# Gamma and beta as PSUM rows, a shared adapter bank, and one instruction list per engine for layer 0 and the seam

## What is computed

```python
# layer 0: adapter of the batch's language, then LayerNorm with its gamma and beta
h = relu(x @ W1[lang] + b1[lang]); v = x + h @ W2[lang] + b2[lang]
c = (v - mean(v)) * rsqrt(var(v) + 1e-5) * gamma[lang] + beta[lang]
x = x + bitlinear(gelu(bitlinear(c, W1f, b1f)), W2f, b2f)      # 256 -> 1024 -> 256
# layer 1: linear of the batch's subject, then a feed-forward with a convolution over tokens
y = x @ W[subj].T + b[subj]
x = x + bit_linear(silu(conv3(bit_linear(y, w1)) + conv_b), w2)
# bitlinear: W -> clip(round(W / mean|W|), -1, 1) * mean|W|; x -> round(x * 127 / max|x|) * max|x| / 127
```

## Time and profile before

| what | us |
|---|---|
| median of 3 runs | 321.74 |
| lowest and highest | 318.56 and 323.08 |
| span of the profiled execution | 319.6 |
| VectorE busy | 276.6 |
| TensorE busy (matmul) | 264.5 |
| GpSimd busy | 259.2 |
| ScalarE busy | 240.6 |

### The profile page before, as it was taken

The page is one execution under the profiler, slowest core; times in us unless marked ns, Lnnn a source line. Parts: engine busy times, 40 slices in busy tenths (PEclk is TensorE's granted clock), DMA queues, the critical chain, the costliest instruction groups (busy, mean ns, idle before and its releaser), DMA issues. The chain is left out here.

```text
span 319.6 us, 6460 instructions
## 1 busy us (share of the span) xinstructions
PE 264.5 (83%) x1676; PEld 179.7 (56%) x1700; DVE 276.6 (87%) x606; ACT 240.6 (75%) x366; POOL 259.2 (81%) x402
## 2 busy tenths in 40 slices
PE   6679878869798887999889797989899898967574
PEld 6234334535455454566656665868587686745452
DVE  0778988896899989955899999999999999999671
ACT  4588897966776487567566888889989888978770
POOL 2567899996898988759999999998989799898310
PEclk9977799999999999999999999999999999999997
DMA  7995773579496368454430333445436373444764
GB/s 249 320 363 118 222 197 76 113 159 213 100 215 126 75 87 178 69 100 91 44 66 2 60 74 66 118 98 91 111 93 122 70 98 82 101 98 100 120 145 115
DMA packets 90745, 39.50 MB, mean 124 GB/s; under 512 B 73005, under 2 KB 88141, under 8 KB 90710
## 3 DMA queue, kind: packets, MB, share of 16 engines
q1 hardware_dynamic: 84532, 30.47, 46.8%
q10 hardware_dynamic: 6178, 8.62, 8.6%
HBM read 18.11 MB, written 4.19 MB: 70 GB/s over the span
## 5 line engine op out<-in xcount | busy, mean ns | idle before, releaser
L812 POOL TENSOR_TENSOR raw_all<-raw_all,mid 128x1024 f32<-128x1024 f32 x32 | 63.7, 2000 | 0.7 <-DVE raw_all L1025 0.7
L548 ACT ACTIVATE g<-banks,dqz 128x1024 f32<-128x1024 f32 x32 | 35.5, 1112 | 24.4 <-POOL r L757 21.2
L805 POOL TENSOR_SCALAR mid<-apad,taps,convb 128x512 f32<-128x512 f32 x64 | 48.8, 774 | 0.5 <-DVE apad L1018 0.5
L608 ACT ACTIVATE banks<-apad,taps 128x512 f32<-128x512 f32 x64 | 42.3, 682 | 6.9 <-DVE apad L1018 6.8
L970 DVE TENSOR_REDUCE am<-g 128x1 f32<-128x1024 f32 x32 | 38.6, 1211 | 8.6 <-ACT g L548 8.5
L1025 DVE SCALAR_TENSOR_TENSOR raw_all<-apad,taps,banks 128x512 f32<-128x512 f32 x64 | 45.8, 743 | 0.0
L1018 DVE TENSOR_TENSOR apad<-banks,dqb 128x512 f32<-128x512 f32 x64 | 40.9, 684 | 4.6 <-PE banks L1337 4.5
L757 POOL TENSOR_SCALAR r<-g,qs 128x1024 uint16<-128x1024 f32 x32 | 36.8, 1153 | 6.2 <-DVE qs L982 5.9
L1365 PE MATMUL banks<-tern,q1T 128*128 128x256 bf16 x256 | 33.8, 276 | 9.5 <-DMA q1T<-r 8.0
L1227 PE MATMUL banks<-tern,qT 128*128 128x512 bf16 x117 | 36.6, 388 | 5.5 <-ACT qcT L540 3.3
L627 ACT ACTIVATE r<-g,qs 128x1024 uint16<-128x1024 f32 x32 | 36.6, 1144 | 5.3 <-DVE qs L1044 3.2
(11 more groups left out here) (116 smaller groups left out, 561.5 us busy)
## 6 DMA issues: line engine op xcount, KB each, us to landing
out_y<-xs SPq DMA_DIRECT2D x32, 128.0 KB, 2.0
xs<-in_x ACTq DMA_DIRECT2D x7, 512.0 KB, 5.7
x2T<-in_xT ACTq DMA_DIRECT2D x4, 512.0 KB, 5.2
wl<-in_cwl SPq DMA_DIRECT2D x8, 256.0 KB, 2.7
xT<-in_xT ACTq DMA_DIRECT2D x3, 512.0 KB, 4.2
raw_all<-in_w1a ACTq DMA_DIRECT2D x1, 1024.0 KB, 5.0
cw<-in_cw SPq DMA_DIRECT2D x16, 64.0 KB, 5.0
gam<-in_gamma SPq DMA_DIRECT2D x8, 128.0 KB, 3.0
```

Of the source, the lines that this page charges most:

```text
L608: act.activation(bank(BANK_U[g % 3]), apad[:, f, 2:S + 2], ACT.Copy, scale=taps[:, f, 2:3]).then_inc(p_last, 1)
L805: pool.tensor_scalar(mid[f // 2 % 2][:, f % 2, :], apad[:, f, 1:S + 1], taps[:, f, 1:2], convb[:, f:f + 1], ALU.mult, ALU.add).then_inc(p_ ...
L812: pool.tensor_tensor(c[:, 2 * q:2 * q + 2, :], c[:, 2 * q:2 * q + 2, :], mid[q % 2][:, :, :], ALU.add).then_inc(p_sum, 1)
```

## The change

1. Gamma and beta. The two tables (10 languages by 256) are loaded once into SBUF (load_affine), with the ids on 10 partitions (load_langs). VectorE compares the ids with a row number (choose_languages). TensorE's affine_columns multiplies the tables by the chosen columns, ScalarE copies the result to affineT, and for each batch TensorE's affine_rows transposes a broadcast column into one PSUM bank (BANK_GB, 7), from which centre and normalise read gamma and beta. The bank has one buffer: affine_rows(b) waits for normalise(b-1,1), and centre waits for affine_rows.
2. The adapter. adapter_in writes to BANK_AD, too, and waits for add_adapted of both pairs of the batch before (until now for the relu alone).
3. scale_z is two operations of one element instead of one of two elements with a stride.
4. Order. Layer 0, the seam and the first batches of layer 1 are one list for each engine (first); slot2 has a new order and runs for s = 3 to 8; the rest is a list (ending). The orders of all engines are new throughout.

```diff
-        gam = [sb(f"gam{k}", [P, D]) for k in range(2)]
-        bet = [sb(f"bet{k}", [P, D]) for k in range(2)]
+        affine = sb("affine", [L, 2, D])
+        affineT = sb("affineT", [P, 2 * KD, B])
+        row_of = sb("row_of", [L, 1])
+        langs = sb("langs", [L, B], I32)
+        chosen = sb("chosen", [L, B])
...
-        amz = [sb(f"amz{k}", [P, 2, 2])[:, :, 0] for k in range(2)]
-        sz = [sb(f"sz{k}", [P, 2, 2])[:, :, 0] for k in range(2)]
+        amz = [sb(f"amz{k}", [P, 2]) for k in range(2)]
+        sz = [sb(f"sz{k}", [P, 2]) for k in range(2)]
...
-        BANK_AD, BANK_DN, BANK_QT, BANK_UP, BANK_IN = 0, 1, 2, 3, 7
+        BANK_AD, BANK_DN, BANK_QT, BANK_UP, BANK_GB = 0, 1, 2, 3, 7
+        columns = bank(BANK_GB)[:, 0:2 * KD * B].rearrange("p (c b) -> p c b", b=B)
+        gam = bank(BANK_GB)[:, 0:D]
+        bet = bank(BANK_GB)[:, D:2 * D]
...
-        def run(opening, slot1, closing, slot2):
-            opening()
-            for s in range(5, B + 1):
-                slot1(s)
-            closing()
-            for s in range(3, B + 4):
+        def run(first, slot2, ending):
+            first()
+            for s in range(3, B + 1):
                 slot2(s)
+            ending()
...
-            def load_norm(b):
...
+            def load_langs():
+                sp.dma_start(langs[:, :], t["ids0"].to_broadcast([L, B])).then_inc(s_langs, 16)
+
+            def load_affine():
+                sp.dma_start(affine[:, 0, :], t["gamma"]).then_inc(s_ldgb, 16)
+                sp.dma_start(affine[:, 1, :], t["beta"]).then_inc(s_ldgb, 16)
...
             def slot2(s):
...
+                on(store2, s - 7, 3)
+                on(store2, s - 6, 1)
+                on(store2, s - 5, 0)
+                on(store2, s - 5, 2)
+                on(transpose2, s - 1, 3)
+                on(transpose2, s, 0)
+                on(transpose2, s, 1)
+                on(transpose2, s, 2)
...
+            load_langs()
+
+            def first():
+                load_adapter_weights(0); load_table(); load_weights(1); load_weights(2); load_second(0); load_ids()
+                load_weights(3); load_first_tokens(); load_affine(); load_adapter_weights(1); load_second(1)
...
+            def ending():
+                store2(2, 3); store2(4, 0); store2(3, 1); store2(4, 2); store2(3, 3); store2(5, 0); store2(5, 2)
+                store2(4, 1); store2(4, 3); store2(5, 1); store2(5, 3); store2(6, 1); store2(6, 0); store2(6, 2)
+                store2(7, 0); store2(6, 3); store2(7, 1); store2(7, 2); store2(7, 3)
...
+            def affine_columns():
+                act.wait_ge(s_gbc, 1)
+                act.activation(affineT[:, :, :], columns, ACT.Copy).then_inc(s_gbT, 1)
...
+            def first():
+                load_tokens(1); weight_sum(0); identities(); load_rows(1); bias_leading(); adapter_hidden(0)
+                load_rows(2); affine_columns(); weight_sum(1); squares(0, 0); squares(0, 1); adapter_hidden(1)
+                bias_middle(); load_rows(3); scaled_weights(1); load_tokens(2); round_z(0, 0); squares(1, 0)
+                untranspose_z(0, 0); round_z(0, 1); squares(1, 1); ternary(1); adapter_hidden(2); gelu(0, 0)
...
+            pool.iota(row_of[:, :], pattern=[[0, 1]], base=0, channel_multiplier=1,
+                      allow_small_or_imprecise_dtypes=True).then_inc(s_rowof, 1)
...
+                bias_table(); negative_mean(0, 0); bias_rest(); negative_mean(0, 1); inverse_deviation(0, 0)
...
+            def choose_languages():
+                dve.wait_ge(s_langs, 16)
+                dve.wait_ge(s_rowof, 1)
+                dve.tensor_scalar(chosen[:, :], langs[:, :], row_of[:, 0:1], None, ALU.is_equal).then_inc(s_chosen, 1)
...
             def centre(b, p):
                 dve.wait_ge(s_nmean[p], b + 1)
-                dve.wait_ge(s_ldgb[b % 2], 32 * (b // 2 + 1))
+                dve.wait_ge(s_gb, b + 1)
...
-                                                   in1=gam[b % 2][:, :], op0=ALU.add, op1=ALU.mult)
+                                                   in1=gam, op0=ALU.add, op1=ALU.mult)
...
-                                                   in1=bet[b % 2][:, :], op0=ALU.mult, op1=ALU.add)
+                                                   in1=bet, op0=ALU.mult, op1=ALU.add)
...
-                dve.tensor_scalar(sz[p], amz[p], QEPS, 1.0 / QMAX, ALU.max, ALU.mult).then_inc(s_sz, 1)
+                for k in range(2):
+                    ins = dve.tensor_scalar(sz[p][:, k:k + 1], amz[p][:, k:k + 1], QEPS, 1.0 / QMAX, ALU.max, ALU.mult)
+                ins.then_inc(s_sz, 1)
...
+            def first():
+                choose_languages(); weight_scale(0); ternary(0); add_adapted(0, 0); centre(0, 0); add_adapted(0, 1)
+                weight_scale(1); normalise(0, 0); absmax_z(0, 0); centre(0, 1); scale_z(0, 0); inverse_z(0, 0)
...
+            def affine_columns():
+                pe.wait_ge(s_ldgb, 32)
+                pe.wait_ge(s_chosen, 1)
+                for c in range(2 * KD):
+                    ins = pe.matmul(columns[:, c, :], affine[:, c // KD, (c % KD) * P:(c % KD + 1) * P], chosen[:, :],
+                                    start=True, stop=True)
+                ins.then_inc(s_gbc, 1)
+
+            def affine_rows(b):
+                if b == 0:
+                    pe.wait_ge(s_gbT, 1)
+                    pe.wait_ge(s_ldid, 16)
+                wait(pe, s_z, pair(b - 1, 1))
+                for c in range(2 * KD):
+                    ins = pe.transpose(bank(BANK_GB)[:, c * P:(c + 1) * P],
+                                       affineT[:, c, b:b + 1].to_broadcast([P, P]), id32[:, :])
+                ins.then_inc(s_gb, 1)
...
             def adapter_in(b):
                 par = b % 2
                 pe.wait_ge(s_ldT[par], 32 * (b // 2 + 1))
-                wait(pe, s_relu, b)
+                wait(pe, s_xx, pair(b - 1, 1))
...
+            def first():
+                weight_total(0); adapter_in(0); affine_columns(); adapter_out(0, 0); affine_rows(0); adapter_out(0, 1)
+                adapter_in(1); weight_total(1); adapter_out(1, 0); adapter_out(1, 1); transpose_z(0, 0)
...
```

More of the change, by code:

```diff
@@ L235, in bank_x @@
         def bank_x(b):
-            return BANK_IN if b == 0 else 0
+            return 0
         def bank_y(b):
-            return BANK_AD if b == 0 else 2
+            return BANK_GB if b == 0 else 2
         BANK_U = [3, 4, 7]
@@ L451, in _ @@
+            def ending():
+                store2(2, 3); store2(4, 0); store2(3, 1); store2(4, 2); store2(3, 3); store2(5, 0); store2(5, 2)
+                store2(4, 1); store2(4, 3); store2(5, 1); store2(5, 3); store2(6, 1); store2(6, 0); store2(6, 2)
+                store2(7, 0); store2(6, 3); store2(7, 1); store2(7, 2); store2(7, 3)
+            run(first, slot2, ending)
             sp.wait_ge(p_st[0], 32 * B)
@@ L677, in _, with ending @@
+            def ending():
+                silu(6, 3); round2(6, 2); silu(7, 0); round2(6, 3); silu(7, 1); round2(7, 0); silu(7, 2); round2(7, 1)
+                silu(7, 3); round2(7, 2); round2(7, 3)
+            run(first, slot2, ending)
         @block.gpsimd
@@ L896, in _, with ending @@
+            def ending():
+                scale_of_down(6, 2); scale_of_down(6, 3); scale_of_down(7, 0); scale_of_down(7, 1)
+                scale_of_down(7, 2); scale_of_down(7, 3)
+            run(first, slot2, ending)
         @block.vector
@@ L1083, in slot2 @@
-            def slot2(s):
+            def slot2(s):
+                on(scale2, s - 3, 1)
+                on(final2, s - 4, 2)
+                on(first_tap, s - 2, 6)
+                on(dequant, s - 2, 7)
+                on(inverse2, s - 3, 1)
+                on(absmax2, s - 3, 2)
+                on(first_tap, s - 2, 7)
+                on(dequant, s - 1, 0)
+                on(final2, s - 4, 3)
+                on(dequant, s - 1, 1)
+                on(scale2, s - 3, 2)
+                on(first_tap, s - 1, 0)
+                on(dequant, s - 1, 2)
+                on(inverse2, s - 3, 2)
+                on(absmax2, s - 3, 3)
+                on(first_tap, s - 1, 1)
+                on(dequant, s - 1, 3)
+                on(first_tap, s - 1, 2)
+                on(scale2, s - 3, 3)
+                on(absmax_y, s)
@@ L1170, in weight_total @@
                 if n >= 2:
-                    wait(pe, s_relu, len(batches))
+                    wait(pe, s_xx, pair(len(batches) - 1, 1))
                     totals.append(n)
@@ L1243, in down1 @@
                 ins.then_inc(s_dn, 1)
-            def slot1(s):
-                on(adapter_in, s)
-                on(up1, s - 3, 3)
-                on(transpose_z, s - 2, 0)
-                once(s, B, transpose_x, 0, 0)
-                on(adapter_out, s, 0)
-                on(down1, s - 4, 3)
-                once(s, B, transpose_x, 0, 1)
-                on(up1, s - 2, 0)
-                on(down1, s - 3, 0)
-                on(transpose_z, s - 2, 1)
```

(10 more changed lines are left out.)

481 lines of the change are left out of this document (202 added, 279 removed).

## The result

| | us |
|---|---|
| before, median of 4 runs (range) | 321.59 (318.56 to 323.08) |
| after, median of 4 runs (range) | 342.16 (341.85 to 344.12) |
| ratio after / before, 95% interval | 1.067 (1.059 to 1.075) |
| profiled execution after: its own time, span | 342.19, 340.4 |

The change makes the kernel 6.7% slower, 340.4-319.6=20.8 us by the spans. The forecast was 320.7 with a range of 309 to 331, so it was wrong, and outside its range. What failed most was the term for layer 1, which the prediction put at 0: it measured +8.0 us; the opening and the end came out 5.5 and 4.2 us above their terms.

What follows compares the result with a forecast made beforehand. Layer 0 was taken to have no single limit (VectorE, GpSimd and TensorE close together), layer 1 to be bound by VectorE. 319.6+11-9-6+3=318.6, plus 2.1 around the span, gave 320.7 us, range 309 to 331.

Steps and rivals of the forecast that it cites:

- the term for layer 1: Layer 1's rearranged slots: VectorE busy 109.3 of 110 us, so nothing to win; 0.
- the opening: Start, up to gelu(1,0): tokens and gamma/beta tables land later behind weight loads, so gelu(1,0) begins near 61; +11 us.
- the end: After the last transpose: 19 stores stand behind it on SP instead of 3; +3 us.
- relief let through in layer 0: Layer 0 after 50 us: TensorE and GpSimd let through three quarters of VectorE's remaining 12 us relief; -9 us.
- longer lists, seam and layer 1: Longer lists recover 6 us of VectorE's idle time in the seam and elsewhere after 50 us; layer 1 itself 0.
- the stretches: VectorE's centring, normalising and scale, lengthened by exclusion with GpSimd, return to unstretched times; 17.9 us together with issue gaps.
- rival 3: VectorE's lengthened operations have another source and stay so; time also 330 us; chance 5%.
- four small products, ScalarE's copy and the adapter's product: Opening chain after gamma and beta land at 24 us; puts the first adapter sum at about 25.5 us.
- VectorE's weight_scale(1) is part of the price: Opening: weight_scale(1) stands ahead of normalise(0,0) and waits behind adapter_in(1); first normalising near 32.5 us.
- 0.4 us a store: End: assumed SP issue time per store, giving 10.8 us after the last transpose's issue, +3.2 us.
- Rival 2: Single buffers make batches wait, 1.3 us in each of seven, 9 us, cancelling the relief; time 330.7 us; chance 22%.
- my sign: Test against single-buffer waits: TensorE's waits for z and xx under 3 us in all; over 8 would mean they bite.

Runs made afterwards that it cites:

- e1: Changed kernel with SP's opening list alone reordered: second adapter weights, gamma/beta and batch 0's tokens issued ahead of the three big weight loads; 329.76 us, ratio to before 1.030.
- e1b: e1 with weight 1's steps moved back behind the first normalising on three engines and affine_columns behind adapter_out(0,0); 332.42 us.
- h1: Changed kernel's operations in the instruction lists of the kernel before, with table loads, column products and row transposes put in; 320.29 us, ratio to before 0.998.
- e8: New lists with the loads of e1, but every layer 1 operation, stores and transposes included, in the old order; 322.69 us, ratio 1.004.
- e13: Changed kernel with e1's loads and e2's stores, plus VectorE's final2(s-3,0) and dequant(s-1,4) ahead of absmax_y; 322.03 us, slots 19.07.
- e2: Changed kernel with SP's stores spread over layer 1's slots, one behind each transpose, so 8 instead of 19 stand behind the last transpose; 336.27 us.
- h4: h1 with both sums of batch 0 ahead of rows and centring, and ScalarE's column copy and squares(0,0) ahead of bias_middle; 315.80 us, ratio 0.985.
- e3: Changed kernel with linear(s,1) ahead of down2(s-3,0) in TensorE's layer 1 slot; 346.45 us.
- e6: Changed kernel with transpose_y, lead_q and first_tap moved earlier in the layer 1 slot on TensorE, ScalarE and VectorE; 347.37 us, slots of 20.02.
- h2: h1 with only one of four row pieces transposed per batch from batch 1 on, 21 TensorE transposes fewer; 318.79 us, ratio 0.989.

## Why the prediction was wrong, by its own steps

| term | predicted | measured |
|---|---|---|
| opening, at gelu(1,0) | +11 | +16.5 |
| relief let through in layer 0 | -9 | -8.2 |
| longer lists, seam and layer 1 | -6 and 0 | -2.7 and +8.0 |
| end | +3 | +7.2 |
| sum | -1 | +20.8 |

The terms that failed are layer 1 at 0, the opening and the end; the seam's gain was half of what I gave it.

**The relief was right**, in mechanism and size: the stretches went (rival 3 falls), VectorE has 13.3 us less (I had 14.2-1.2=13.0, without the gaps), a batch takes 14.38 us where I said 14.3, TensorE is busy 83.8 of 90 us between 60 and 150, or 93%. TensorE's row transposes were 5.9 us busy in all, not 4, which this sum did not feel. The read from PSUM costs nothing, as the rows had it: 474 to 476 ns where the unstretched was 476 to 482. The Trainium skill's fixed part of 120 cycles against 58 (VectorE: DVE Perf Modes, "The TRN2 errata") would have shown as an estimated 65 ns more in each of 64 operations, at the 0.96 GHz of the same table (4 us in all, the estimate of the prediction); it doesn't, and the measurement decides.

**The opening was right in kind, mis-sized.** I had the gamma table at 24 and the first sum at 25.5; the product that needs the table started at 25.70 and the sum at 29.61. The step that failed is "four small products, ScalarE's copy and the adapter's product": this chain took 3.9 us, not 1.5. At full clock its two products took 1.05 and 1.13 us (e1), so 1.8 of the 2.4 us are the clock granted behind the idling, which I had not priced there; 1.7 us more came from the load. From the first sum to gelu(0,0) were 20.1 us where I had 17.5, and from there to gelu(1,0) 16.8 where I had 17.8. Carrying the lateness through to the end was right: e1's 13.8 us at gelu(1,0) are 13.7 at the last tap. My reading that VectorE's weight_scale(1) is part of the price was not borne out (e1b). The cause is the place of the loads in SP's list, shown by e1: it alone is worth 12.4 us.

**"Layer 1's slots are rearranged, but at 109.3 of 110 there is nothing to win: 0"** is the step that failed most. Nothing to win is not nothing to lose. An engine that is busy for 109.3 of 110 us has nothing to give, so a new order could hardly gain and could well add, and I should have bounded that term from above; a slot 0.93 us longer, seven times, is 6.5 of the 8.0 us. Shown: the order costs it (h1, e8: 18.3 with the same operations). Not settled: which link. Two were named and taken away together (e13) for 0.28 us of the 0.9. That several run side by side from absmax_y to TensorE is argued from the waits; GpSimd's wait for scale_y, still there, was not tried.

**"The longer lists: I give them 6"** was 6 us for a list being longer, without a mechanism. The seam gave 2.7; in h1, with the old lists, it gave 0.2.

**The end was mis-sized.** I took 0.4 us a store, nearest the shortest issue; 19 took 9.44, so 0.50 each. With 0.5 my sum gives 1.3+0.6+17x0.5+2.1=12.5 behind the issue of the transpose, where 13.6 were measured. But 19 stores leave 18 steps and not 17, the transpose's own issue took 2.27 us, and nothing lay between it and the stores, so 2.3+18x0.5+2.1=13.4. This part is 6.0 of the 7.2 us. The other 1.2 lie ahead of the last transpose, where the four stores, listed in the diff, stand that I had not counted at all. e2 shows the cause: 5.9 us. Rival 2's sum has 4 us for the end where the forecast has 3, a slip of 1 us.

**Rival 2** (single buffers) is right in one place: TensorE's waits for z and the adapter's sums are 3.8 us in all in the kernel after (my sign said under 3), 2.6 and 1.0 of them in the opening, none over 0.2 later. There it costs, if h4 is read rightly. In the batches, where I had priced it at 1.3 us each, no such wait is seen.

## What to carry to other kernels

Time lost ahead of the first product can arrive at the end undiminished (13.8 us in, 13.7 out, with TensorE 93% busy in between), so put what the first result needs ahead of every big load, and price the chain behind an idle TensorE at the low clock. It need not: the kernel before turned 2.5 us at gelu(1,0) into 0.5 at gelu(7,0) between its two profiles. A rearranged slot around a full engine shouldn't be put at "0": look on every engine for what stands behind a waiting operation, and multiply one wait by the number of slots. Where taking a wait away only moves it, compare whole orders, seam and slot together, instead of swapping neighbours.

## What was not expected of the hardware

- The issue of one 512 KB load held SP's queue for 5.10 us in the kernel after while weight loads before it were under way (0.40 in the kernel before, 0.39 in e1 with the same load further ahead, in both ahead of those loads). It shows again in the profiles of e2, e3 and e6, which have the same list: 4.87, 6.35 and 4.40 us. Whether the 3 MB issued ahead of it are what counts was not tried.
- A store's issue took 0.57 us in the median before and 0.45 after, where many stand in a row.
- TensorE lost 21 transposes in h2, and three batches at full clock took 42.41 us instead of 42.45, though TensorE was the busiest engine of layer 0 in h1, 90.9 of 100 us.
- The same product of the adapter took 1.13 us at a granted clock of 1.00 and 2.07 at 0.50, behind 12 us of idling.
